# Feature sums of a graph network: the tile table with six columns, and the base copied at a tile's head

## What is computed

```python
x = x + L0(h, edge_attr_16, src, dst, ...)   # two rounds of messages and a GRU
x = x + L1(h, edge_index, ...)               # graph convolution, degrees of dst
x = x + L2(h, edge_index, edge_attr_16, ...) # mean, and the last edge's features
x = x + L3(h, edge_index, edge_attr_32, ...) # edge network and a GRU
# in L0: a = segment_sum(concat(hv[dst], hv[src], e) @ W_msg + b_msg, dst)
# in L1: deg = segment_sum(ones, dst)
# in L2: out = out.at[dst].set(edge_attr @ W_e + b_e)   (the last edge of a node wins)
```

## Time and profile before

| | us |
|---|---|
| median of 3 runs | 5971.55 (5969.33 to 5974.3) |
| the profiled execution | 5953.41 |
| its span, first to last instruction | 5951.6 |
| feature sums, about 47 to 560 us of the span | 513 |
| build of the adjacency tiles, to about 1910 us | 1350 |
| the dense products of four layers, to about 3258 us | 1348 |
| edge network and the last GRU | 2693 |

### The profile page before, as it was taken

The page is one execution under the profiler, slowest core; times in us unless marked ns, Lnnn a source line. Parts: engine busy times, 40 slices in busy tenths (PEclk is TensorE's granted clock), DMA queues, the critical chain, the costliest instruction groups (busy, mean ns, idle before and its releaser), DMA issues. The chain is left out here.

```text
span 5951.6 us, 110293 instructions
## 1 busy us (share of the span) xinstructions
PE 3693.0 (62%) x30524; PEld 2706.8 (45%) x30525; DVE 2642.5 (44%) x7089; ACT 1102.8 (19%) x2165; POOL 2142.3 (36%) x2644
## 2 busy tenths in 40 slices
PE   3454067667776979899898244444454555554557
PEld 3443012222222979898897233333333343443346
DVE  5445777666665553312323133333333333343335
ACT  1222013445666012200011000000000000000002
POOL 4554800000000020111101666566656565565550
PEclk5555598888776999999998555555555555555557
DMA  2000000000111524354543122222222222222221
GB/s 118 0 0 0 3 11 23 33 33 39 45 50 78 197 71 152 133 175 157 178 152 111 41 54 53 52 56 54 56 56 54 55 60 56 56 60 55 57 56 32
DMA packets 173664, 404.77 MB, mean 68 GB/s; under 512 B 47902, under 2 KB 109481, under 8 KB 172809
## 3 DMA queue, kind: packets, MB, share of 16 engines
q1 hardware_dynamic: 52409, 259.35, 12.3%
q10 hardware_dynamic: 69360, 91.59, 5.7%
q0 software_dynamic: 51680, 51.82, 5.1%
HBM read 359.52 MB, written 43.07 MB: 68 GB/s over the span
## 5 line engine op out<-in xcount | busy, mean ns | idle before, releaser
L695 POOL DMA_INDIRECT scr<-ptable,src_i x1566 | 1530.3, 977 | 1024.4 <-POOLq L693 564.0
L664 POOL COPY late<-late 128x256 f32<-128x256 f32 (+1 forms) x65 | 26.0, 400 | 2263.8 <-POOLq L662 2263.8
L970 PE MATMUL ps_g<-arena 128*128 128x192 bf16 x1854 | 410.0, 353 | 461.0 <-issue 454.2
L1037 PE MATMUL ps_zz<-scr,arena 128*128 128x192 bf16 x7203 | 612.4, 247 | 65.7 <-PEq L1035 65.7
L1037 PEld LDWEIGHTS ps_zz<-scr,arena 128*128 128x128 fp8e4 x7203 | 601.1, 99 | 75.6 <-issue 73.5
L904 ACT ACTIVATE arena<-arena 128x384 f32<-128x384 f32 x309 | 161.6, 523 | 2433.3 <-ACTq L903 1999.8
L1640 DVE TENSOR_TENSOR arena<-arena 128x196 int32 x1350 | 480.1, 356 | 7.2 <-issue 7.2
L970 PEld LDWEIGHTS ps_g<-arena 128*128 128x128 bf16 x1854 | 236.1, 140 | 508.8 <-issue 499.0
L1145 PE MATMUL ps_zz<-arena,cand 128*128 128x392 fp8e4 x784 | 242.2, 398 | 331.9 <-PEq L1143 194.9
L958 PE MATMUL ps_zz<-sb_w_e,arena 64*128 64x128 f32 x930 | 278.8, 434 | 245.3 <-issue 238.1
L1037 PE MATMUL ps_zz<-arena 128*128 128x192 bf16 x4802 | 406.2, 247 | 24.1 <-PEq L1035 24.1
(11 more groups left out here) (395 smaller groups left out, 5986.1 us busy)
## 6 DMA issues: line engine op xcount, KB each, us to landing
arena<-a_dram SPq DMA_DIRECT2D x245, 784.0 KB, 4.3
arena<-low_dram ACTq DMA_DIRECT2D x309, 192.0 KB
a_dram<-arena SPq DMA_DIRECT2D x49, 784.0 KB, 3.3
arena<-in_e32g ACTq DMA_DIRECT2D x309, 96.0 KB
scr<-ptable,src_i POOLq DMA_INDIRECT x1566
arena<-in_e16p SPq DMA_DIRECT2D x1, 13387.5 KB, 35.4
x<-in_x_nm SPq DMA_DIRECT2D x1, 1664.0 KB, 8.7
out_nm<-x SPq DMA_DIRECT2D x1, 1664.0 KB
```

The source lines that it names most:

```text
L695: pool.indirect_dma_start(grow[:, g % RING, j, :], None, ptable, bass.IndirectOffsetOnAxis(ap=src_i[:, g * GC + j:g * GC + j + 1], axis=0) ...
L970: last = pe.matmul(ps_d[:, m % 2, 0:3 * H], masks[:, m, :, j], msg_h[:, m, j, :, :], start=j == 0, stop=j == GC - 1)
L1037: last = pe.matmul(ps_z[b % 2][:, 0:3 * H], amat[b][:, i, :], hsp[k % 2][:, i, :], start=(i == 0), stop=(i == NT - 1))
```

## The change

The table loses column 6, which nothing read, and its row is now six numbers (24 bytes where it was 28): column 0 is the running sum, 1 the number of groups of the branch not taken, 2 `lo`, 3 `ng`, 4 `nr`, 5 `n0`. In the feature sums ScalarE now loads columns 2 to 5 (4 registers for 6), GpSimd 2 and 3 (2 for 4), VectorE's `stats_tile` 2 to 4 (3 for 5) and `stats_end` column 4 alone (1 for 5). TensorE loads 1 as before. VectorE copies the base at the head of the tile, ahead of the addition to `itiles`, and no longer in `stats_end`; where `nr` is over 1, `stats_end` loads `lo` by itself inside the branch. One cast that filled column 6 is gone. Other edits belong to the branch that doesn't run.

```diff
-        tile_tab = sb("tile_tab", [1, NT + 1, 7], i32)
+        tile_tab = sb("tile_tab", [1, NT + 1, 6], i32)
...
-            lim = [(0, CH - 1), (1, GMAX), (0, NT * GMAX), (1, SMAX), (1, RBMAX), (1, RBG), (0, CH - 1)]
+            lim = [(0, NT * GMAX), (1, GMAX), (0, CH - 1), (1, SMAX), (1, RBMAX), (1, RBG)]
...
             with pool.Fori(0, NT) as t:
-                lo, _, _, ng = load_range(pool, t, (0, 1, 2, 3))
+                lo, ng = load_range(pool, t, (2, 3))
...
             with act.Fori(0, NT) as t:
-                lo, _, _, ng, nr, n0 = load_range(act, t, (0, 1, 2, 3, 4, 5))
+                lo, ng, nr, n0 = load_range(act, t, (2, 3, 4, 5))
...
-            v.tensor_copy(tile_tab[:, 0:NT - 1, 6], rowp[:, 1:NT, 0])
...
             def stats_end(t, i):
 
-                lo, _, _, _, nr = load_range(v, t, (0, 1, 2, 3, 4))
+                (nr,) = load_range(v, t, (4,))
                 v.wait_ge(s_st, 1)
...
-                v.tensor_copy(base[:, ds(t, 1)], cidx[:, ds(lo, 1)])
 
                 with v.If(v.snap(nr - 1)):
+                    (lo,) = load_range(v, t, (2,))
                     v.wait_ge(s_rawc, 1)
...
             def stats_tile(t, before_it):
 
-                lo, _, _, ng, nr = load_range(v, t, (0, 1, 2, 3, 4))
+                lo, ng, nr = load_range(v, t, (2, 3, 4))
+                v.tensor_copy(base[:, ds(t, 1)], cidx[:, ds(lo, 1)])
                 link(v.tensor_scalar(itiles[:, :, :], itiles[:, :, :], float(P), None, ALU.add))
```

More of the change, by code:

```diff
@@ L458, in load_windows, with load_range @@
             return [(k % GF, GF + k % 2, k, *vals[k::WT]) for k in range(WT)]
-        def load_range(eng, t, which=(0, 1)):
-            lim = [(0, CH - 1), (1, GMAX), (0, NT * GMAX), (1, SMAX), (1, RBMAX), (1, RBG), (0, CH - 1)]
+        def load_range(eng, t, which=(1, 2)):
+            lim = [(0, NT * GMAX), (1, GMAX), (0, CH - 1), (1, SMAX), (1, RBMAX), (1, RBG)]
             k0, k1 = which[0], which[-1] + 1
@@ L636, in spread @@
                 with pool.Fori(0, NT) as t:
-                    lo, ng = load_range(pool, t)
+                    ng, lo = load_range(pool, t)
                     with pool.Fori(0, ng) as g:
@@ L921, in spread @@
             def spread(k):
-                total = pe.value_load(tile_tab[0:1, NT:NT + 1, 2], min_val=0, max_val=NT * GMAX)
+                total = pe.value_load(tile_tab[0:1, NT:NT + 1, 0], min_val=0, max_val=NT * GMAX)
                 first = pe.snap(total * k * big)
@@ L927, in spread @@
                     (ng,) = load_range(pe, t, (1,))
-                    before = pe.value_load(tile_tab[0:1, ds(t, 1), 2:3].rearrange("o w a -> o (w a)"), min_val=0, max_val=NT * GMAX)
+                    before = pe.value_load(tile_tab[0:1, ds(t, 1), 0:1].rearrange("o w a -> o (w a)"), min_val=0, max_val=NT * GMAX)
                     pe.wait_ge(s_accf, 1)
@@ L1333, in spread @@
                 with v.Fori(0, NT) as t:
-                    lo, ng = load_range(v, t)
+                    ng, lo = load_range(v, t)
                     link(v.tensor_scalar(itile[:, :], iota_h[:, 0:P], tbase[:, ds(t, 1)], None, ALU.add))
@@ L1720, in _ @@
             v.tensor_copy(tile_tab[:, 0:NT, 3], rowi[:, 0, 0:NT])
-            v.tensor_copy(tile_tab[:, 0:NT, 0], rowp[:, 0:NT, 0])
+            v.tensor_copy(tile_tab[:, 0:NT, 2], rowp[:, 0:NT, 0])
             v.tensor_copy(tile_tab[:, 0:NT, 1], rowi[:, 1, 0:NT])
-            v.tensor_copy(tile_tab[:, 1:NT + 1, 2], rowf[:, 3, 0:NT])
-            v.tensor_copy(tile_tab[:, 0:NT - 1, 6], rowp[:, 1:NT, 0])
+            v.tensor_copy(tile_tab[:, 1:NT + 1, 0], rowf[:, 3, 0:NT])
             link(v.tensor_copy(tile_tab[:, 0:NT, 4], rowi[:, 3, 0:NT]))
```

## The result

| | before | after |
|---|---|---|
| median of 6 runs each, us | 5972.93 (5968.01 to 5980.6) | 5948.35 (5938.25 to 5954.92) |
| the profiled execution | 5953.41 | 5954.92 |

The ratio is 0.9958, with a 95% interval from 0.9945 to 0.997: 24.6 us faster. Repeated twice on other occasions it was 0.9965 (0.9952 to 0.9979) and 0.9965 (0.9952 to 0.9978), 18.2 and 21.6 us between the medians. One run of the kernel before on the first of these occasions took 6076.75 us at a mean granted clock of 0.631, where the others have 0.673 to 0.677, and is left out. The mean of the three is 21.5 us, where 29 were predicted.

A forecast was written before the change was run, and what follows sets the result against it. The feature sums were taken as a ring of waits, not one full engine. Terms 4.6 + 17 + 3 + 3 + 1.4 gave 29 us, median 5971.5 to 5942.5; range 5931 to 5961.

The forecast's parts named there:

- a ring of waits: Feature sums, 513 us: no engine busy over 285, so what they give up comes off the kernel's end.
- The price of the loads: Table loads: 0.3 us for the first register, 0.2 each further; four for one price at multiples of 16 bytes.
- The odd tiles, 17 us: Heads of odd tiles 9 to 47: ScalarE and GpSimd load sooner, TensorE starts earlier; 0.85 us each in 20 tiles.
- the lateness: VectorE late for a tile's second group, 0.38 us in tile 15; shorter end load and moved copy remove it.
- The step that failed: Tile 15's head: GpSimd's second subtraction ends 0.19 us after the second one-hot, at 314.50, so TensorE starts 0.77 us earlier.
- Tiles 9, 13, ..., 45: Odd tiles with a one in front (13, 17, 21, ...): no lateness to lose, gain about 0.8 us each.
- the rule of the Trainium skill: VectorE and GpSimd lock shared ports, so start order decides; if GpSimd only slowed, odd tiles give about 5 us less.
- Tiles 10, 14, ... and 12, 16, ...: Even tiles from 10: first kind gains 0.46 us each, 4.6 in all; second 0.3 each, 3 in all.
- Every register costs 0.2 us: Rival, chance 0.17: table loads have no short address; odd tiles give 11 us for 17, total 23, 5948.5 us.
- The ring closes elsewhere: Rival, chance 0.12: shorter heads meet TensorE's head or the base copy; 0.2 us a tile, 10 us, 5961.5.
- The slower kernel: Rival, chance 0.03: the build's mean clock falls to 0.77, adding 43 us; kernel 14 us slower, 5985.5.

The follow-up runs named there:

- off8: Changed kernel with eight-column table, needed numbers in columns 1 to 4, so no load starts at a multiple of 16 bytes; sums 489.8 us against about 489.
- align8: Changed kernel with eight-column table, needed four first, all head loads four registers at multiples of 16 bytes; sums 477.0 and 477.4 us, ratio 0.9944 to before.
- end5: Changed kernel with the `stats_end` load back to five registers; sums 510.1 us, against about 489 for the changed kernel and 510.9 before.

## Why the prediction was right, and where its sizes were off

**What bounds the kernel** was read rightly. The stage is a ring of waits, and what it gave up came off the end: 21.8 us in the stage, 21.5 as the mean over the three pairs of medians.

**The price of the loads.** "About 0.3 us for the first and 0.2 for each further one", and four for one price from an address that 16 divides: ScalarE 0.31 and 0.91 us (forecast 0.32 and 0.95), GpSimd 0.52 (0.52), VectorE's head 0.76 (0.74) and end 0.31 (0.30). off8 and align8 confirm the address from both sides. The Trainium skill, Runtime: NRT & Kernel Launch, section "Instruction fetch mechanics", gives about 200 ns per register. The steps between the loads that are not short agree (0.30, 0.52, 0.76 and 0.91 us for one to four registers), and the 0.31 us for four registers at a multiple of 16 bytes do not; here the measurement decides.

**The odd tiles, 17 us, measured 13.7.** Right in the mechanism: GpSimd slips into the first one-hot, the lateness goes. The step that failed is "at 313.91, the second subtraction starts ... and ends 0.19 after the second one-hot". It does end 0.19 after it, but the second one-hot itself ends later. GpSimd's first subtraction ends 0.19 us behind the first one-hot (309.14 against 308.95), so that VectorE's pair of one-hots takes 1.43 us for 1.28 before. I moved GpSimd and left VectorE where it was, though the two wait for each other both ways. This is 0.13 us in the way of the sums, and VectorE's head gained 0.17 us (from the end of tile 14's last one-hot to the first of 15: 2.18 before, 2.01 after) and not 0.23 (0.24 by the prediction's own terms). So TensorE's sums came 0.56 us sooner and not 0.77.

The missing 3.3 us don't lie evenly. Tiles 11, 15, ..., 47 gained 0.83 us each, close to the forecast; tile 27 gained 0.81 for 0.85. Tiles 9, 13, ..., 45 were put down as "about 0.8" and gained 0.54, which is 2.6 of the 3.3. They have no lateness to lose, so the step above is all of their gain: 0.57 in tiles 13 and 21. And in tiles 9 and 17 there was no turn to win. GpSimd's first subtraction stood inside the first one-hot before the change too, 0.54 us behind its start, and took 0.36; these two gained 0.32. The prediction worked out tiles 15 and 27 and took the others for like them.

A reading of its rows was wrong as well. One-hots of 0.69 us are not those "beside GpSimd": tile 14's first takes 0.69 with GpSimd idle, and those of tile 16 take 0.56 with GpSimd at work beside them. It is a property of the tile, the same in both kernels, and no run shows its cause. Nothing in the sum hung on it.

Beside this stands the rule of the Trainium skill that the prediction weighed (SBUF — State Buffer, section "SBUF: two separate sides": VectorE, in some modes, and GpSimd lock their shared ports for a whole instruction). The traces agree in what it makes of the times. The subtraction takes 0.36 us alone; where it starts in a one-hot it takes up to 0.89, and in nearly all cases of all 14 profiles it ends 0.19 to 0.22 us behind that one-hot, whenever it began. A GpSimd that only ran slower would not end at a fixed distance. The 0.19 are less than the 0.36 of its own work, though, so it isn't blocked from its very start.

**Tiles 10, 14, ... and 12, 16, ...** 3.8 for 4.6 and 2.4 for 3. Right in direction and place. The head of tile 16 in after:

```profile
319.01 0.45 PE L1199 MATMUL ps_g<-stat_w 128*128 128x51 bf16 x6 [0.44 <-PEq L1197]
...
319.97 0.56 DVE L1796 TENSOR_TENSOR stat_w<-dst_s,itiles 128x768 bf16<-128x768 int16 x1 [1.67 <-DVEq L1793]
```

The second group follows the sums (end 319.46) by 0.51 us, where it was 1.01. The lateness of 0.5 is gone. But the prediction had VectorE's longer head covered by waits, and it wasn't: from tile 15's last one-hot to tile 16's first, start to start, it is 2.18 us where it was 1.94. Tile 16 kept 0.35 of the 0.5, the ten tiles on average 0.24.

**Tile 0** stood in no term of the sum, since no instruction of its groups changed. It lost 1.8 us. This is a part that no reading of the changed instructions would give: a pause of VectorE's sequencer stands at another instruction, and the loop runs in its slower order.

**The rivals.** "Every register costs 0.2 us" fell by ScalarE's 0.31 us and by off8, though its time (5948.5) is nearest of all to the measured median of 5948.35: its 23 us came from a wrong price and a wrong account of the odd tiles. "The ring closes elsewhere" fell in its form here (0.2 us a tile, 10 us), but end5 shows that such a ring exists: with the end's load long, the shorter heads give 0.8 us of 21.9, and 2.7 of 8.3 in the ten tiles where the comparison is fair. The slower kernel did not come: the build's mean granted clock stayed between 0.80 and 0.82, and the way from line 1820 to the first gather was 2709 to 2719 us for before, after and variants alike on the chips that need about 5950 us.

## What to carry to other kernels

Before adding up what several shorter steps give, ask for each whether another one of the list covers it: here the parts alone gave 0.8 and 8.6 us and the whole 21.9. Where two engines hold each other up, as VectorE and GpSimd do here, work out both engines' new times and not just those of the one that was moved, and look at more than one or two turns of the loop. The order of two starts can be worth more than the length of a small operation: a copy of 0.15 us made the stage 8.9 us shorter at the head of a tile than behind group 0. Put what a loop loads from a table at a multiple of 16 bytes and in four neighbouring numbers, load all four even where two are wanted, and look for the gain in the stage itself where the rest of the kernel scatters by more.

## What the runs showed of the hardware

**A load of registers costs by its address.** One register 0.30 us, two 0.52, three 0.76, four 0.91 to 0.95, five 1.18, six 1.33. From a multiple of 16 bytes: two 0.52, three 0.76, four 0.31 to 0.32, five 0.59, six 0.76. So four go as one, further ones are added, and two or three gain nothing.

**A loop with two rhythms.** Tile 0's groups, from the third on, took 2.57 us on average in both executions of before, and 2.65 in all twelve others, with the same instructions. A single pause of 0.47 us in VectorE's sequencer, one instruction sooner or later, goes with the one or the other.

**The same gathers, another chip.** One chip ran all four kernels sent to it, and the kernel before, in 5318 to 5347 us. Its feature sums took as long as elsewhere (align8 477.0 and 477.4). Most of the difference lies in the edge network. From 3300 to 5200 us, in before and then in align8 on that chip:

```profile
3300.00:5200.00 1900.00, 915.32 (x6527) 690.69 (x6528) 661.27 (x1741) 114.06 (x218) 1152.19 (x1179) 0.50 0.24 54
```

```profile
3300.00:5200.00 1900.00, 1114.16 (x8857) 912.48 (x8858) 905.32 (x2363) 154.20 (x295) 1445.16 (x1493) 0.50 0.31 72
```

The granted clock is 0.50 in both, and the DMA engines move 72 GB/s for 54. The gathers, in the page of before and in that of align8 (busy us, mean ns of one, idle before them and its releaser):

```profile
L695 POOL DMA_INDIRECT scr<-ptable,src_i x1566 | 1530.3, 977 | 1024.4 <-POOLq L693 564.0
```

```profile
L695 POOL DMA_INDIRECT scr<-ptable,src_i x1566 | 1517.0, 969 | 482.0 <-issue 398.5
```

GpSimd spends the same time on issuing them and is idle 540 us less before them; 480 of these are waits at line 693 (564.0 us, and 83.5 there). From the first gather to the last it is 1993.1 us there and 2549.2 in before. Why the transfers land sooner there was not tried, and all of it comes from one occasion on that chip. For a comparison it means that times from two chips must not be put beside each other.
